# Twelve tables through one-hot lookups instead of eleven, gathers paced by TensorE's matmuls, and a batch tile's pairwise products issued in one piece

## What is computed

```python
e = stack([tbl_f[ids[:, f]] for f in range(26)], axis=1)          # 512 x 26 x 128
combined = concatenate([dense[:, None, :], e], axis=1)            # 512 x 27 x 128
inter = einsum('bnd,bmd->bnm', combined, combined)                # 27 x 27 per sample
z = concatenate([dense, inter[:, triu_i, triu_j]], axis=1)        # 128 + 351
h = concatenate([z, dense], axis=1)                               # 607
h = maximum(h @ W_top1 + b_top1, 0)                               # 512
h = maximum(h @ W_top2 + b_top2, 0)                               # 256
y = h @ W_top3                                                    # 1
```

## Time and profile before

| | |
|---|---|
| time, median of three runs | 105.53 us |
| the three runs | 105.53, 104.25, 107.01 us |
| span of the profiled execution | 141.4 us |
| mean granted TensorE clock in it | 0.855 |
| TensorE busy (matmuls) | 105.4 us, 1525 matmuls |
| VectorE / ScalarE / GpSimd busy | 52.7 / 48.3 / 60.9 us |
| DMA | 13.46 MB, 95 GB/s |

### The profile page before, as it was taken

How to read it: one execution, slowest core, us unless ns; L and a number is a source line. 1 busy time by engine, 2 the same in 40 slices (tenths; PEclk the granted TensorE clock), 3 DMA queues, 4 the chain that set the end, 5 groups by cost and what they waited for, 6 DMA issues and landing times.

```text
span 141.4 us, 3474 instructions
## 1 busy us (share of the span) xinstructions
PE 105.4 (75%) x1525; PEld 85.9 (61%) x1525; DVE 52.7 (37%) x116; ACT 48.3 (34%) x82; POOL 60.9 (43%) x66
## 2 busy tenths in 40 slices
PE   6999899999979960366795223441997999967993
PEld 2476678788858950164684122221996998957980
DVE  2999999699279800000050000000043034103210
ACT  4749929597079520201023000000105106310342
POOL 1887877478567775705227777770000000000000
PEclk9999999999999997558689555555599999998699
DMA  4899999999992122100101122220000000000000
GB/s 131 282 234 256 264 262 234 249 241 234 305 381 71 51 60 55 38 19 23 37 5 48 48 59 57 56 56 19 0 5 5 5 5 0 0 5 5 5 0 1
DMA packets 5365, 13.46 MB, mean 95 GB/s; under 512 B 1731, under 2 KB 1991, under 8 KB 5222
## 3 DMA queue, kind: packets, MB, share of 16 engines
q1 hardware_dynamic: 3260, 9.11, 24.1%
q0 software_dynamic: 1920, 3.94, 10.8%
q10 hardware_dynamic: 170, 0.18, 0.4%
HBM read 13.23 MB, written 0.00 MB: 94 GB/s over the span
## 4 chain that ended last, share of the span: by engine, by line
PE 65%; issue 23%; DVE 6%; ACT 2%; DMA 2%; DVEq 0%
PE ps_a L334 27%; PE ps_gram L371 11%; PE ps_a L420 9%; DVE onehot L560 5%; PE ps_h L434 5%; PE ps_rows L349 4%; PE ps_a L410 3%; PE ps_a L397 2%; DMA idrow<-ids_by_table 2%; PE ps_rows L447 1%; ACT xt L659 1%; DVE part_sb L569 1%; PE ps_h L460 1%; ACT table_sb L666 1%; PE ps_gram L390 0%
## 5 line engine op out<-in xcount | busy, mean ns | idle before, releaser
L307 POOL DMA_INDIRECT rows_sb<-tbl,ids_sb x60 | 60.5, 1009 | 34.1 <-issue 16.5
L334 PE MATMUL ps_a<-onehot,part_sb 125*128 125x512 f32 (+1 forms) x208 | 46.9, 376 | 2.9 <-issue 2.6
L334 PEld LDWEIGHTS ps_a<-onehot,part_sb 125*128 125x128 f32 x208 | 35.8, 197 | 11.2 <-issue 3.4
L371 PE MATMUL ps_gram<-xt 128*27 128x27 f32 x1024 | 16.9, 205 | 22.5 <-issue 21.6
L371 PEld LDWEIGHTS ps_gram<-xt 128*27 128x27 f32 x1024 | 13.5, 118 | 27.1 <-issue 25.1
L560 DVE TENSOR_SCALAR onehot<-idrow,row_id 125x1024 fp32r<-125x1024 int16 (+1 forms) x42 | 27.7, 712 | 4.9 <-remote 3.3
L608 DVE TENSOR_SCALAR table_sb<-ps_a,columns_sb 128x128 f32<-128x128 f32 x8 | 2.4, 347 | 43.7 <-PE ps_a L420 39.5
L420 PE MATMUL ps_a<-table_sb,w_sb 128*128 128x128 f32 x72 | 13.0, 326 | 6.8 <-issue 6.4
L652 ACT COPY xt<-ps_a 128x512 f32<-128x512 f32 (+1 forms) x13 | 7.5, 575 | 31.1 <-PE ps_a L334 18.9
L587 DVE STREAM_TRANSPOSE table_sb<-ps_gram 128x864 f32<-128x864 f32 x4 | 4.3, 1084 | 32.3 <-PE ps_gram L371 32.3
L420 PEld LDWEIGHTS ps_a<-table_sb,w_sb 128*128 128x128 f32 x72 | 11.2, 232 | 7.6 <-issue 6.9
(11 more groups left out here) (35 smaller groups left out, 46.0 us busy)
## 6 DMA issues: line engine op xcount, KB each, us to landing
table_sb<-tbl SPq DMA_DIRECT2D x11, 448.0 KB
idrow<-ids_by_table SPq DMA_DIRECT2D x5, 256.0 KB
w_sb<-w SPq DMA_DIRECT2D x1, 1280.0 KB, 8.7
rows_sb<-tbl,ids_sb POOLq DMA_INDIRECT x60
table_sb<-tbl SPq DMA_DIRECT2D x10, 52.0 KB
w_sb<-w SPq DMA_DIRECT2D x1, 512.0 KB
dense_sb<-dense_by_column SPq DMA_DIRECT2D x1, 256.0 KB
idrow<-ids_by_table ACTq DMA_DIRECT2D x1, 128.0 KB
```

The lines of the kernel that those rows point to most:

```text
L307: pool.indirect_dma_start(rows_sb[:, t % ROWS_RING, k, :], None, tables[f], bass.IndirectOffsetOnAxis(ids_sb[:, t, f:f + 1], 0),).then_inc ...
L334: last = pe.matmul(ps_a[:, i % 2, a:b], parts_sb[part][:, w, c * D:(c + 1) * D], unit_onehot(u, c)[:, member, a:b], start=(part == HIGH an ...
L371: last = pe.matmul(ps_gram[j * NPAD:j * NPAD + N, half, s * N:(s + 1) * N], x, x, start=True, stop=True)
```

## The change

1. Table 0, of 1,250 rows, moves from the gathered ones to the looked-up ones, between table 24 and table 25, with 10 rows on each of 125 partitions: a unit of its own with a chunk count of 10. The groups of gathered tables shrink from 4, 4, 4, 3 to 4, 4, 4, 2, and gathers from 60 to 56. The looked-up tables are twelve, with ten lookups of the whole batch and four of halves.
2. Every gather from the seventh on waits for a count that TensorE raises in the middle of its program (`gathers_paced`): three places in each whole lookup, one in each of the first two half lookups (32 places), and from there one place for each two gathers at blocks of the layers: the first matmul of `layer1_dense(t, 0)` for t < 3 and the first of `layer1_pairs(t, 0)` and `layer1_pairs(t, 2)`, nine places in all.
3. The four quarters of `gram(1)` and of `gram(2)` stand together, ahead of all of `layer1_pairs` and `layer2` of the tile before. (Those of tile 3 stood together before.) VectorE's order becomes pack 0, pack 1, relu1_high 0, pack 2, relu1_high 1, relu1_high 2, pack 3, relu1_high 3.

```diff
@@ -27,15 +27,15 @@
 
 
 
-ONEHOT_TABLES = [4, 10, 11, 17, 19, 20, 24, 25, 3, 8, 14]
+ONEHOT_TABLES = [4, 10, 11, 17, 19, 20, 24, 0, 25, 3, 8, 14]
 VP = 125
-CHUNKS = [8] * 11
+CHUNKS = [8] * 7 + [10] + [8] * 4
 CH = max(CHUNKS)
 SIZES = sorted(set(CHUNKS))
 FIRST_COLUMN = {c: sum(x + 1 for x in SIZES if x < c) for c in SIZES}
 ROW_COLUMNS = sum(c + 1 for c in SIZES)
 
-UNITS = [[0], [1, 2], [3, 4], [5, 6], [7, 8], [9, 10]]
+UNITS = [[0], [1, 2], [3, 4], [5, 6], [7], [8, 9], [10, 11]]
 UNIT_OF = [u for u, members in enumerate(UNITS) for _ in members]
 COMPARED = [CHUNKS[members[0]] - 1 for members in UNITS]
 BEFORE_UNIT = [sum(COMPARED[:u]) for u in range(len(UNITS))]
@@ -69,19 +69,35 @@
 GATHERED = [f for f in range(F) if f not in ONEHOT_TABLES]
 ORDER = [0] + [f + 1 for f in ONEHOT_TABLES] + [f + 1 for f in GATHERED]
 FIRST_GATHERED = 1 + NOH
-GROUP_SIZES = [4, 4, 4, 3]
+GROUP_SIZES = [4, 4, 4, 2]
 GROUP_STARTS = [sum(GROUP_SIZES[:i]) for i in range(len(GROUP_SIZES))]
 GROUPS = [(t, i, k) for t in range(TILES) for i, k in zip(GROUP_STARTS, GROUP_SIZES)]
 assert sum(GROUP_SIZES) == len(GATHERED)
 
-AFTER_LOOKUP = [[], [], [], [0], [1], [2], [3], [4], [5], [6], [7]]
+AFTER_LOOKUP = [[], [], [], [0], [1], [2], [3], [4], [5], [6], [7], []]
 LOOKED_UP_BESIDE = sum(len(gs) for gs in AFTER_LOOKUP)
 assert sum(AFTER_LOOKUP, []) == list(range(LOOKED_UP_BESIDE)) and len(AFTER_LOOKUP) == FIRST_HALF_UP_TO
 GROUPS_UP_TO = [sum(t <= tile for t, _, _ in GROUPS) for tile in range(TILES)]
 
 WARM_UP = 13
-GATHERS_PER_LOOKUP = 3
 GATHERS_AHEAD = 6
+PACES_PER_LOOKUP, PACES_PER_HALF = 3, 1
+PACES_BESIDE = PACES_PER_LOOKUP * (NOH - 2) + PACES_PER_HALF * 2
+
+
+def paces_in(matmuls, paces):
+
+    return [matmuls * (k + 1) // paces - 2 for k in range(paces)]
+
+
+def pace_of(gather):
+
+    behind = gather + 1 - GATHERS_AHEAD
+    if behind <= PACES_BESIDE:
+        return behind
+    return PACES_BESIDE + -(-(behind - PACES_BESIDE) // 2)
+
+
 HIGH, LOW = PARTS = range(2)
 
 
@@ -187,6 +203,7 @@
         dense_copied = sem("dense_copied")
         distance_ready = sem("distance_ready")
         part_ready = [sem(f"part{i}_ready") for i in PARTS]
+        gathers_paced = sem("gathers_paced")
         lookup_done = sem("lookup_done")
         lookup_copied = sem("lookup_copied")
         group_turned = sem("group_turned")
@@ -301,9 +318,8 @@
                 for k in range(first, first + n):
                     f = GATHERED[k]
                     issued = t * len(GATHERED) + k
-                    if issued >= GATHERS_AHEAD and (issued - GATHERS_AHEAD) % GATHERS_PER_LOOKUP == 0:
-                        lookups = (issued - GATHERS_AHEAD) // GATHERS_PER_LOOKUP + 1
-                        pool.wait_ge(lookup_done, min(lookups, len(LOOKUPS)))
+                    if issued >= GATHERS_AHEAD:
+                        pool.wait_ge(gathers_paced, pace_of(issued))
                     pool.indirect_dma_start(
                         rows_sb[:, t % ROWS_RING, k, :], None, tables[f],
                         bass.IndirectOffsetOnAxis(ids_sb[:, t, f:f + 1], 0),
@@ -316,6 +332,8 @@
                 h, a, b = LOOKUPS[i]
                 w, chunks, u = h % WORK_RING, CHUNKS[h], UNIT_OF[h]
                 member = h - UNITS[u][0]
+                paces = PACES_PER_LOOKUP if b - a == B else PACES_PER_HALF if i < FIRST_HALF_UP_TO else 0
+                paced_at = paces_in(2 * chunks, paces)
                 if i >= 2 and 0 in quarters:
                     pe.wait_ge(lookup_copied, i - 1)
                 for half in range(2):
@@ -334,6 +352,9 @@
                             last = pe.matmul(ps_a[:, i % 2, a:b], parts_sb[part][:, w, c * D:(c + 1) * D],
                                              unit_onehot(u, c)[:, member, a:b], start=(part == HIGH and c == 0),
                                              stop=(part == LOW and c == chunks - 1))
+                            place = half * chunks + part * (chunks // 2) + c - half * chunks // 2
+                            if place in paced_at:
+                                last.then_inc(gathers_paced, 1)
                 if 3 in quarters:
                     last.then_inc(lookup_done, 1)
 
@@ -407,8 +428,10 @@
                 if t:
                     pe.wait_ge(h1_high_ready if k else h1_low_ready, t)
                 for m in range(2 * k, 2 * k + 2):
-                    pe.matmul(h1_block(t, m), w1d[:, m * P:(m + 1) * P],
-                              dense_sb[:, t * P:(t + 1) * P], start=(m % 2 == 0), stop=False, skip_group_check=True)
+                    first = pe.matmul(h1_block(t, m), w1d[:, m * P:(m + 1) * P],
+                                      dense_sb[:, t * P:(t + 1) * P], start=(m % 2 == 0), stop=False, skip_group_check=True)
+                    if m == 0 and t < TILES - 1:
+                        first.then_inc(gathers_paced, 1)
 
             def layer1_pairs(t, m):
 
@@ -419,6 +442,8 @@
                 for c in range(ZC):
                     last = pe.matmul(h1_block(t, m), w1_sb[:, c, m * P:(m + 1) * P],
                                      zt[:, t % 2, c, :], start=False, stop=(c == ZC - 1), skip_group_check=True)
+                    if c == 0 and m % 2 == 0:
+                        last.then_inc(gathers_paced, 1)
                 if m % 2:
                     last.then_inc(h1_done, 1)
 
@@ -486,15 +511,11 @@
             layer1_dense(0, 1)
             turn_z(0)
             turn_group(9)
-            gram(1, 0)
-            layer1_pairs(0, 0)
-            layer1_pairs(0, 1)
-            gram(1, 1)
-            layer1_pairs(0, 2)
-            layer1_pairs(0, 3)
-            gram(1, 2)
+            for q in range(QUARTERS):
+                gram(1, q)
+            for m in range(M1):
+                layer1_pairs(0, m)
             layer2(0, 0)
-            gram(1, 3)
             layer2(0, 1)
             layer1_dense(1, 0)
             layer1_dense(1, 1)
@@ -502,15 +523,11 @@
             turn_z(1)
             turn_group(11)
 
-            gram(2, 0)
-            layer1_pairs(1, 0)
-            layer1_pairs(1, 1)
-            gram(2, 1)
-            layer1_pairs(1, 2)
-            layer1_pairs(1, 3)
-            gram(2, 2)
+            for q in range(QUARTERS):
+                gram(2, q)
+            for m in range(M1):
+                layer1_pairs(1, m)
             layer2(1, 0)
-            gram(2, 3)
             layer2(1, 1)
             layer1_dense(2, 0)
             layer1_dense(2, 1)
@@ -524,10 +541,8 @@
             layer2(2, 0)
             turn_group(15)
             layer1_dense(3, 0)
-            gram(3, 0)
-            gram(3, 1)
-            gram(3, 2)
-            gram(3, 3)
+            for q in range(QUARTERS):
+                gram(3, q)
             layer2(2, 1)
             layer1_dense(3, 1)
 
@@ -610,10 +625,10 @@
                 last.then_inc(h1_high_ready, 1)
 
             pack(0)
+            pack(1)
             relu1_high(0)
-            pack(1)
+            pack(2)
             relu1_high(1)
-            pack(2)
             relu1_high(2)
             pack(3)
             relu1_high(3)
```

## The result

The kernel after takes 116.13 us (median of four runs, 114.3 to 117.52), the kernel before, run beside it, 105.75. The ratio is 1.095, 95% interval 1.080 to 1.110: slower by 10.4 us, where 5.9 had been forecast, and 0.6 us above the stated range.

A forecast was written before the change was run, and what follows sets the result against it. TensorE, 75% busy and full in the lookups, was taken to bound the kernel. Terms 4.6 - 0.4 + 0.3 + 0 + 1.9 + 2.0 - 2.5 = +5.9 on 105.5 gave 111.4 us, range 102.8 to 115.5.

The forecast's parts named there:

- Base: Whole kernel before: 141.4 us profiled less stalls gives 99.2 us, so at most 6 of 42 us stalls are in timed runs.
- The 3.2 us of tile 3: Tile 3's products and the layer behind: a 2.11 us hole and eight matmuls in 1.78 instead of 1.06 us.
- stalls beside gathers: TensorE's stops while GpSimd issues gathers: some 3 us of them expected in a timed run.
- Twelfth table, +4.2 and +0.3: Lookups: 20 more matmuls +4.6 us, four transposes fewer -0.4; VectorE and ScalarE work for it +0.3.
- Places in the lookups, 0: Gathers paced within lookups stay about as continuous as before: 0, with a gain or loss of 0.5 us.
- Places in the layers, +1.9: Last four gathers land late, so `turn_group(14)` and `(15)` wait 1.1 and 1.2 us: +1.9 us, bounds 0.5 and 3.
- Products in one piece, +2.0: Tiles 1 and 2: products use up instructions faster than they load, 1.0 us each; bounds nothing and twice 2.11.
- Relief, -2.5: Products beside gathers: holding gathers to the layers removes most of 3 us of timed stalls, -2.5 us.
- Rival C: Both instruction holes, late last gathers and late one-hots in full, no relief: 117.8 us, chance 0.13.
- A: Gather stalls are the larger part of the timed run and go: faster, 103.4 us or down to 102, chance 0.18.
- B: A draw: lookup costs 4.2, relief gives 3, instruction loading hides, last gathers cost 1: 107.7 us, chance 0.22.
- D: Pacing does nothing, GpSimd always behind its permission, neither relief nor tail: 112.0 us; chance 0.47 together with the forecast.

The follow-up runs named there:

- the second profile: The kernel before, unchanged, profiled once more; measured time 106.33 us, span 104.4 us.

## Why the prediction was right or wrong

**Base.** Reading the first profile's 42 us of stalls as not being in a timed run was right, and the rebuilt 99.2 us holds: the second profile has 104.4, which is 5.2 more, and 2.31 + 0.61 us of it are stops at block ends. The 3.2 us of tile 3 add up to 2.8 by their rows (2.11 and 1.78 - 1.06), and the second part was no stall: the first profile's clock fell at 129.6 us, amid that layer. Calling 3 us of the rest "stalls beside gathers" was a guess; slower products come to 1.5 us at most.

**Twelfth table, +4.2 and +0.3.** 4.2 us in the lookups is right (3.8 to 4.3), and VectorE hid its part. Net it cost 2.2, in good part since it moves the block ends of all that follows (4.0 with the ends put back, the difference being only half seen in the traces). The step that failed is not the price but that I weighed block ends only for the products in one piece, not for the instructions that the table adds.

**Places in the lookups, 0.** Right.

**Places in the layers, +1.9.** Right mechanism and place, wrong size: 4.8 us by the ratios of the kernels with and without them (1.095 and 1.050), 4.1 with the products in quarters (1.061 and 1.022). GpSimd's last gathers after, start us and us, show the term:

```profile
84.23 0.94 POOL L323 DMA_INDIRECT rows_sb<-tbl,ids_sb  x1 [5.63 <-PE ps_a L443]
85.48 0.94 POOL L323 DMA_INDIRECT rows_sb<-tbl,ids_sb  x1 [0.30 <-issue]
...
95.47 0.95 POOL L323 DMA_INDIRECT rows_sb<-tbl,ids_sb  x1 [0.30 <-issue]
```

The place is the first matmul of `layer1_pairs(1, 0)` at 82.97. I had allowed 0.4 us from a release to its gather; here it is 1.26, against 0.30 between two gathers in line. And all ten last gathers run back to back from there: 11.24 us to the last one's start and 2.57 to its landing (chain of waits; I had 2.25). 1.26 + 11.24 + 2.57 = 15.1 us, while TensorE, unhindered, needs 92.78 - 81.44 = 11.3 from that matmul to its last group. 3.8 us is what is missing, and the three waits add up to 3.9.

The step that failed is that groups 8 to 13 were called covered and only the last four gathers were followed. The last gather of `turn_group(13)` was to have landed 4.8 us behind `layer1_pairs(1, 2)`, with the group wanted at 5.4. It starts at 87.97, lands 2.50 us later at 90.47, which is 6.0 us behind that block (84.4), and TensorE had come to the group at 89.43, 5.0 us behind it. With the products in quarters and the same places the group doesn't wait: in one piece, `layer1_pairs(1, 0)` and `(1, 2)` stand only 1.5 us apart. Behind T (91.07) the forecast was near: the last two gathers start at T + 3.16 and T + 4.40 (T + 2.9 and T + 4.15), and `turn_group(14)` and `(15)` wait 2.7 us together, where 1.1 + 1.2 = 2.3 had been worked out; the recorded +1.9 is that sum with too short a way (0.7 us, here 1.0) from the last landing to tile 3's products. The late groups also deepen tile 3's stop, as shown above, by 0.8 to 1.5 us.

**Products in one piece, +2.0.** Mechanism and place right, about 1 us too small: 2.9 us by the ratios without places in the layers (1.022 to 1.050), 3.6 with them. The holes of 2.0 and 2.2 us were the upper bound that I had halved. On the kernel before it costs 1.2%, at most 2.6, so its price seems to hang on where blocks end. The Trainium skill's rule ("Runtime: NRT & Kernel Launch", Instruction fetch mechanics), that crossing a block is mostly hidden, holds in tiles 1 and 2 with quarters between layers (no stop, or one of 0.21 us) and fails at 256 products in a row; that blocks are of 256 instructions, two stops exactly 128 products apart bear out.

**Relief, -2.5.** Failed outright: 0 (three gathers at each place against free gathers, 1.049 and 1.050). The long stalls belonged to one execution. What is left of the mechanism is there, and is swallowed. Tile 1's first 171 products take 1.86 us in the kernel after, in which GpSimd issues one gather beside them, and 2.76 with free gathers, which follow each other every 1.25 us:

```profile
63.82 2.76 PE L392 MATMUL ps_gram<-xt 128*27 128x27 f32 x171
67.52 1.17 PE L392 MATMUL ps_gram<-xt 128*27 128x27 f32 x85 [0.94 <-issue]
```

But the stop behind them is 2.01 us there and 0.94 here: TensorE goes on 3.87 and 3.70 us after the first product, when its instructions are there, and tile 1's turn takes 12.2 and 12.3 us. With quarters, which have no such stop, places in the layers do shorten that turn, from 11.54 to 10.95 us.

In sum 2.2 + 0 + 2.9 + 4.8 = 9.9 us, of 10.0 by the ratio and 10.4 by the medians. That it comes out is no test, for the terms are steps of one chain of kernels (the table, then one piece, then the places); in the other order the products cost 3.6 and the places 4.1, and each step has an interval of some 2 us. The forecast's +5.9 missed by its relief (2.5), the late gathers (2.9) and the products (0.9), partly cancelled by the table (2.3). Rival C had the two holes and the late tail in full and came nearest, in kind and with its 117.8 us; its late one-hots didn't come. Rivals A, B and D all fell.

## What to carry to other kernels

When a profile shows long waits that the timed runs have no room for, take a second profile before pricing any relief from them. When work is released by places in another engine's program, follow the whole line of releases from the first place whose work runs without a pause, not only the last ones, and add the restart of the idle engine. And small matmuls in a row can outrun the loading of their own instructions: put long ones between them, don't expect faster small ones to help, and distrust a difference of 1 or 2% that a few idle instructions ahead can make or undo.

## What the runs showed of the hardware that was not expected

TensorE's stops of up to 2.4 us lie at fixed counts of 256 records, moved by exactly the 64 or 16 matmuls put ahead. All 40 of them end 2.3 to 3.0 us after an instruction packet, so their sizes (0.17 to 2.40 us) follow from when that packet went. With the clock at its lower level behind such a stop, eight layer matmuls took 1.83 us instead of 1.16. 64 products of 27 columns take 0.75 to 1.00 us; 171 in a row took 2.76 us beside gathers that followed each other and 1.86 with a single one; whether gathers are the whole cause isn't shown. A gather released to an idle GpSimd starts 1.26 us after the start of its matmul in `layer1_pairs` and 0.74 after one in `layer1_dense` (63.60 to 64.34), one in line 0.30 after the end of the one ahead. And one execution of the kernel before was stalled by 37 us beside its gathers, as none of the 15 other profiled executions was; why, these runs don't say.
